# Flamingo cross-attention with a mixture-of-experts FFN: PV in pairs, four P buffers, scores apart, V in halves

## Chip, cores and metric

One core of one Trainium2 chip. The metric is the device time of one execution in microseconds (us), as the median of the runs.

## What is computed

Sixteen batch entries of 56 queries attend to 1500 context keys of width 128 in 16 heads of 8 lanes; then a gated residual, and an FFN with 8 routed experts (top 2) and a shared one.

```python
q = layernorm(x) @ qw.T + qb;  k = ctx @ kw.T + kb;  v = ctx @ vw.T + vb      # 16 x 56 x 128, 16 x 1500 x 128
scores = einsum('bhqd,bhkd->bhqk', qh * 8 ** -0.5, kh)
scores = where(mask[:, None] == 0, -1e9, scores)
probs = softmax(scores, axis=-1)
x = x + tanh(g_xattn) * (einsum('bhqk,bhkd->bhqd', probs, vh) @ ow.T + ob)
x = x + tanh(g_ffn) * ffn(layernorm(x))          # out / max(|out|), 8 experts, top 2, and a shared one
```

## The kernel before, in words

The program is a written-out order for each engine, with semaphores between them. The attention runs in units k = -1 to 15, one for each batch entry, and each unit works on three entries at once: keys of entry k+2 (`pe_k`, `pe_any`), scores for the row maximum and V of entry k+1 (`pe_score`, `pe_v`, `pe_max_row`), and transposed scores, exponentials and PV of entry k (`pe_scores_t`, `act_exp`, `pe_pv`). The 1500 keys are twelve tiles of 128 (the last of 92), and a unit has twelve steps j, one a tile. PE's order in a unit is `pe_unit`, ScalarE's (ACT) `act_unit`, VectorE's (DVE) `dve_unit`.

- K: three matmuls of 512, 512 and 476 columns into `misc`, the third bank of `ring`. ACT stores each to `k_raw`, GpSimd splits it in two halves of fp16, DMAs lay them in `keys`. `misc` is used in turn for K (steps 0 to 2), any (3), the spread of the sums (`pe_attn`, step 4) and V (steps 5 to 7), and each waits until the one before it is read out.
- Score: 24 matmuls of 112 x 512 (the last eight of 476), fp16, into banks 0 and 1 of `ring` in turn. DVE takes the maximum over each (`dve_max`), so score m waits for maximum m - 2. `S_STEPS` says how many stand in each step: 2, 2, 2, 2, 2, 3, 3, 3, 3, 2, 0, 0.
- st: eight fp16 matmuls of 112 columns, the transposed scores of one tile. ACT's `act_exp` makes P of it in `probs`, with three buffers before.
- PV: `pe_pv` uses the array as four groups of 32 columns. Heads 3g to 3g+2 go to group g as one matmul of 168 columns (the wide ones, the first loop) and head 12+g as one of 56 (the narrow ones, the second loop), all fp32. The tile of step j is multiplied two steps later (`LAG = 2`), one PV in each step; the last two tiles of entry k stand in steps 0 and 1 of unit k+1.
- After PV of an entry DVE reads it out (`dve_norm`, three instructions, step 2), `pe_attn` spreads the sums, `dve_recip` takes the reciprocal (step 4), GpSimd multiplies. V waits for that reciprocal.

Unit 15 has st and PV alone. Behind it in DVE's queue stand `dve_bias`, `dve_split` for four experts and only then the norm of entry 15, on which the projection waits:

```python
            units(dve, dve_unit, {0: add_bias})
            dve_bias(dve)
            for e in range(EARLY):
                dve_split(dve, e)
            dve_norm(dve, (B, B % NB, B // NB))
            dve_recip(dve, (B, B % NB, B // NB))
```

Of the kernel before, what the change touches and what calls it, by code (L numbers as in the profile page):

```python
# [13 lines left out]
P = 128  # L14
# [4 lines left out]
KT = 12  # L19
# [59 lines left out]
def flamingo_kernel(nc, d, out):  # L79

    with ExitStack() as ctx:
# [37 lines left out]
        sums = sb("sums", [P, 2, S])  # L119
        max_part = sb("max_part", [QW, PAIRS, NCH])  # L120
        neg_max = sb("neg_max", [QW, PAIRS], F16)
        probs = sb("probs", [P, 3, HQ])
        recip = sb("recip", [P, 2, S])
        attn = sb("attn", [P, 2, TOK])
        ow_rows = sb("ow_rows", [P, 2, D])
# [96 lines left out]
            return chunk(c).stop - c * CH  # L222


        S_STEPS, at = [], 0
        for n in (2, 2, 2, 2, 2, 3, 3, 3, 3, 2, 0, 0):
            S_STEPS.append(range(at, at + n))
            at += n
        assert at == PAIRS * NCH
# [39 lines left out]
        def pe_k(pe, b, c):  # L269

            k, u, t = b
            w = buf(b, 2)
            if c == 0:
                pe.wait_ge(ctx_loaded[w], 16 * (lap(b, 2) + 1))
                if not known(k, 0):
# [17 lines left out]
        def pe_attn(pe, b):  # L293

            k, u, t = b
            if has(k, 2):
                pe.wait_ge(s["any_done"], k + 3)
            else:
                pe.wait_ge(s["v_stored"], NCH * (k + 1 if k < B else B))
            pe.wait_ge(s["sums_done"], k)  # L300
            for r in range(2):
                mm = nc.tensor.matmul(misc[:, r * S:(r + 1) * S], spread[:, r, :], sums[:, r, :],
                                      start=True, stop=True)
            mm.then_inc(s["spread_made"], 1)

        def pe_v(pe, b, c):

            k, u, t = b
            if c == 0:
                if has(k, -1):  # L310
                    pe.wait_ge(s["recip_done"], k)
# [9 lines left out]
            mm.then_inc(s["v_made"], 1)  # L321

        def pe_score(pe, b, m):

# [38 lines left out]
        def pe_pv(pe, b, j):  # L363
# [8 lines left out]
            for g in range(CG):  # L372
                rows = slice(CW * g, CW * (g + 1))
                nc.tensor.matmul(pv[rows, 0:HG * S], v_ext[0:m, u, j, VW * HG * g:VW * HG * g + CW],  # L374
                                 probs[0:m, j % 3, HG * S * g:HG * S * (g + 1)],
                                 start=(j == 0), stop=(j == KT - 1), skip_group_check=True)
            for g in range(CG):
                rows = slice(CW * g, CW * (g + 1))
                h = WIDE + g
                mm = nc.tensor.matmul(pv[rows, HG * S:(HG + 1) * S], v_ext[0:m, u, j, VW * h:VW * h + CW],  # L380
                                      probs[0:m, j % 3, S * h:S * (h + 1)],
                                      start=False, stop=(j == KT - 1), skip_group_check=True)
            mm.then_inc(s["pv_done"], 1)

        LAG = 2

        def pe_unit(pe, b):
            k, u, t = b
            before = (k - 1, buf(b, -1), None)
            for j in range(KT):  # L390
                if j in K_STEPS and has(k, 2):
                    pe_k(pe, b, K_STEPS.index(j))
                if has(k, 0):
                    pe_scores_t(pe, b, j)
                scores = list(S_STEPS[j]) if has(k, 1) else []
                for m in scores[0:1]:
                    pe_score(pe, b, m)
# [4 lines left out]
                if j in V_STEPS and has(k, 1):  # L402
                    pe_v(pe, b, V_STEPS.index(j))
                for m in scores[1:2]:
                    pe_score(pe, b, m)
                if j >= LAG and has(k, 0):
                    pe_pv(pe, b, j - LAG)
                if j < LAG and has(k, -1):
                    pe_pv(pe, before, KT - LAG + j)
                for m in scores[2:]:  # L410
                    pe_score(pe, b, m)
                if j == TURN_STEP and has(k, 1):
                    pe_max_row(pe, b)

# [117 lines left out]

        def dve_unit(dve, b):
            k, u, t = b
            for j in range(KT):
                if j == 0 and has(k, 2):
                    dve_mask(dve, b)
                if j == NORM_STEP and has(k, -1):
                    dve_norm(dve, b)
                scores = list(S_STEPS[j]) if has(k, 1) else []  # L540
                for m in scores[0:1]:
                    dve_max(dve, b, m)
                if j == ANY_STEP and has(k, 2):
                    dve_any(dve, b)
                for m in scores[1:2]:
                    dve_max(dve, b, m)
                if j == RECIP_STEP and has(k, -1):
                    dve_recip(dve, b)
                for m in scores[2:]:
                    dve_max(dve, b, m)  # L550
                if j == TURN_STEP - 1 and has(k, 1):
                    dve_merge_max(dve, b)


        def pool_keys(pool, b, c):
# [586 lines left out]
```

## Time and profile before

| | us |
|---|---|
| median of three runs | 580.48 (579.09 to 580.92) |
| the profiled execution | 578.95 |
| its span, first to last instruction | 577.1 |
| attention units, unit 0's first K to the last PV | 57.4 to 450.8 |
| one unit (the turn of the row maxima to the next one) | 25.30 |
| after the attention | 457.2 to 577.1 |

The span is what the profiler saw of one execution; the profiled execution's own time is 1.85 us more. A timeline row gives the start and the length of a run of like instructions; the difference of two starts is what PE took from one to the other. Ends of matmuls overlap the next starts, so starts are compared here and not ends. An fp32 matmul of the program shows as two in the trace.

### The profile page before, as it was taken

What the parts mean: (1) busy time and instruction counts of PE and PEld (TensorE: products, weight loads), DVE (VectorE), ACT (ScalarE), POOL (GpSimd) and SP (SyncE); (2) the same over time, 40 slices, a digit from 0 to 9 for tenths busy, and PEclk for the clock granted to TensorE, in tenths of its full rate; (3) what the DMA queues carried; (4) which work ended last, traced back from release to release, by engine and by line L of the source; (5) the groups of instructions that cost most, each with busy time, mean ns of one, the idle gap of its engine ahead of it and who ended that gap; (6) DMA issues with size and microseconds to landing.
All of it is one profiled execution on the core that took longest, in us unless ns stands there. A gap on an engine that the chain in (4) does not pass through costs nothing.

```text
span 577.1 us, 15690 instructions
## 1 busy us (share of the span) xinstructions
PE 509.8 (88%) x6779; PEld 353.5 (61%) x6779; DVE 399.5 (69%) x753; ACT 330.3 (57%) x411; POOL 140.5 (24%) x128
## 2 busy tenths in 40 slices
PE   1365999999999999999999999999899469999993
PEld 1123667676766767676676767667677355777772
DVE  6357567687766768776776878677674556778756
ACT  2211566656566665656666565665657228788781
POOL 4051514325061432506153250605000000000000
PEclk9869899999999999999999999999999768999997
DMA  4999869886686867668586766847000500210001
GB/s 151 197 246 243 176 167 178 218 184 134 151 190 150 172 152 185 131 153 185 150 173 156 175 136 156 183 84 163 3 3 2 147 0 2 71 42 2 1 2 32
DMA packets 39805, 72.82 MB, mean 126 GB/s; under 512 B 4638, under 2 KB 26271, under 8 KB 39736
## 3 DMA queue, kind: packets, MB, share of 16 engines
q1 hardware_dynamic: 38456, 70.90, 54.1%
q10 hardware_dynamic: 1280, 0.92, 0.7%
q8 instruction: 53, 0.87, 0.7%
q14 instruction: 16, 0.13, 0.1%
HBM read 24.28 MB, written 0.46 MB: 43 GB/s over the span
## 4 chain that ended last, share of the span: by engine, by line
PE 75%; DVE 12%; DMA 5%; issue 4%; ACT 2%; SPq 1%; POOL 1%; ACTq 0%; POOLq 0%; DVEq 0%
PE ring L336 14%; PE pv L374 12%; PE st L357 11%; PE ring L281 9%; PE ring L319 8%; PE st L661 7%; DVE max_part L501 7%; PE ring L700 5%; DMA ctxT<-in_ctx 3%; PE pv L380 3%; DVE recip L530 2%; DMA ident_h<-in_c_ident_h 2%; PE pv L700 1%; SPq L265 1%; PE ring L909 1%
## 5 line engine op out<-in xcount | busy, mean ns | idle before, releaser
L501 DVE TENSOR_REDUCE max_part<-ring 112x1 f32<-112x512 f32 (+1 forms) x384 | 245.3, 673 | 104.2 <-PE ring L336 102.5
L454 ACT ACTIVATE probs<-st 128x896 f32<-128x896 f32 x192 | 175.6, 915 | 104.1 <-PE st L357 101.3
L336 PE MATMUL ring<-keys,qrs 121*112 121x512 f16 (+1 forms) x384 | 141.2, 392 | 8.4 <-DVE max_part L501 4.0
L357 PEld LDWEIGHTS st<-qrs,keys 121*128 121x128 f16 (+1 forms) x1536 | 89.7, 102 | 42.9 <-issue 13.9
L357 PE MATMUL st<-qrs,keys 121*128 121x112 f16 (+1 forms) x1536 | 108.8, 214 | 2.0 <-ACT qrs L443 2.0
L561 POOL TENSOR_TENSOR k_hi<-k_raw,zero 128x512 f16<-128x512 f32 (+1 forms) x45 | 45.9, 1019 | 219.6 <-ACT k_raw L422 219.0
L374 PE MATMUL pv<-probs,v_ext 128*32 128x168 f32 (+1 forms) x1536 | 94.5, 318 | 0.3 <-DVE sums L521 0.2
L281 PE MATMUL ring<-ctxT,w_qkv 128*128 128x512 f32 (+1 forms) x94 | 56.5, 688 | 13.3 <-DMA ctxT<-in_ctx 13.1
L336 PEld LDWEIGHTS ring<-keys,qrs 121*112 121x112 f16 x384 | 46.6, 131 | 32.2 <-DVE max_part L501 26.2
L374 PEld LDWEIGHTS pv<-probs,v_ext 128*32 128x32 f32 (+1 forms) x1536 | 30.3, 108 | 46.3 <-issue 33.8
L422 ACT ACTIVATE k_raw<-ring,biases 128x512 f32<-128x512 f32 (+1 forms) x45 | 30.5, 677 | 46.3 <-PE ring L281 44.7
L683 DVE TENSOR_TENSOR keys<-probs,keys 128x896 f16<-128x896 f32 x36 | 39.3, 1091 | 24.6 <-ACT keys L678 24.5
L319 PE MATMUL ring<-w_qkv,ctxT 128*128 128x128 f32 (+1 forms) x384 | 52.0, 278 | 4.3 <-DVE recip L530 4.3
L319 PEld LDWEIGHTS ring<-w_qkv,ctxT 128*128 128x128 f32 (+1 forms) x384 | 48.9, 189 | 9.1 <-DVE recip L530 8.5
L380 PE MATMUL pv<-probs,v_ext 128*32 128x56 f32 (+1 forms) x1536 | 54.2, 213 | 0.0
L380 PEld LDWEIGHTS pv<-probs,v_ext 128*32 128x32 f32 (+1 forms) x1536 | 50.0, 110 | 4.7
L564 POOL TENSOR_TENSOR k_lo<-k_raw,k_hi 128x512 f16<-128x512 f32 (+1 forms) x45 | 51.1, 1135 | 3.5
L661 PE MATMUL st<-keys 128*128 128x512 f16 x216 | 48.8, 366 | 0.5 <-DVE score L1011 0.5
L670 ACT ACTIVATE probs<-st,up_bias 128x896 f32<-128x896 f32 x36 | 36.2, 1007 | 16.7 <-PE st L661 16.7
L434 ACT ACTIVATE v_ext<-ring 128x512 f32<-128x512 f32 (+1 forms) x48 | 27.4, 571 | 24.1 <-PE ring L319 24.1
L700 PE MATMUL ring<-keys 128*128 128x128 f16 x612 | 40.0, 219 | 0.9 <-DVE keys L683 0.9
L700 PEld LDWEIGHTS ring<-keys 128*128 128x128 f16 x612 | 36.3, 98 | 6.5 <-DVE keys L683 1.0
(113 smaller groups left out, 374.4 us busy)
## 6 DMA issues: line engine op xcount, KB each, us to landing
ctxT<-in_ctx SPq DMA_DIRECT2D x16, 750.0 KB, 4.2
keys<-mask_add SPq DMA_DIRECT2D x32, 375.0 KB
keys<-k_hi SPq DMA_DIRECT2D x32, 375.0 KB, 6.1
keys<-k_lo SPq DMA_DIRECT2D x32, 375.0 KB, 7.0
keys<-mask_add SPq DMA_DIRECT2D x32, 281.2 KB
mask_raw<-in_mask SPq DMA_DIRECT2D x15, 375.0 KB, 3.7
up_w<-in_up_w SPq DMA_DIRECT2D x9, 256.0 KB, 2.8
down_w<-in_down_w SPq DMA_DIRECT2D x9, 256.0 KB, 3.2
```

Source lines behind the costliest of these rows:

```text
L281: nc.tensor.matmul((first_k[c] if known(k, -1) else misc)[:, 0:width(c)], w_qkv[:, 1, :], ctxT[:, w, chunk(c)], start=True, stop=True).the ...
L319: mm = nc.tensor.matmul(misc[0:m, i * P:(i + 1) * P], ctxT[:, buf(b, 1), j * P:j * P + m], w_qkv[:, 2, :], start=True, stop=True)
L336: nc.tensor.matmul(ring[0:QW, m % 2, 0:width(c)], qrs[0:ROWS, w, p, :, :].rearrange("r h q -> r (h q)"), keys[0:ROWS, w, p, chunk(c)], sta ...
L357: mm = nc.tensor.matmul(st[0:m, j % 2, p // 4, QW * (p % 4):QW * (p % 4 + 1)], keys[0:ROWS, u, p, j * P:j * P + m], qrs[0:ROWS, u, p, :, : ...
L374: nc.tensor.matmul(pv[rows, 0:HG * S], v_ext[0:m, u, j, VW * HG * g:VW * HG * g + CW], probs[0:m, j % 3, HG * S * g:HG * S * (g + 1)], sta ...
L380: mm = nc.tensor.matmul(pv[rows, HG * S:(HG + 1) * S], v_ext[0:m, u, j, VW * h:VW * h + CW], probs[0:m, j % 3, S * h:S * (h + 1)], start=F ...
L454: nc.scalar.activation(probs[0:m, j % 3, :].rearrange("p (h c) -> p h c", h=2), st[0:m, j % 2, :, 0:HQ // 2], ACT.Exp).then_inc(s["exps_do ...
L501: nc.vector.tensor_reduce(max_part[:, p, c:c + 1], ring[0:QW, m % 2, 0:width(c)], AX.X, ALU.max).then_inc(s["max_read"], 1)
L561: nc.gpsimd.tensor_tensor(k_hi[:, chunk(c)], k_raw[:, chunk(c)], zero[:, :].to_broadcast([P, width(c)]), ALU.add).then_inc(s["k_hi_made"], 1)
L564: nc.gpsimd.tensor_tensor(k_lo[:, chunk(c)], k_raw[:, chunk(c)], k_hi[:, chunk(c)], ALU.subtract).then_inc(s["k_lo_made"], 1)
L661: mm = nc.tensor.matmul(st[:, n % 2, h, 0:cols], split_w[e][:, 0, w, c * P:(c + 1) * P], xn_p[:, x, 4 * P * h:4 * P * h + cols], start=(i ...
L700: mm = nc.tensor.matmul(down_banks[e % 2][t // 4][:, P * (t % 4):P * (t % 4 + 1)], hid[:, n % HR, x, P * t:P * (t + 1)], split_w[e][:, 1, ...
```

## The change

`probs` gets a fourth buffer. PV is issued two tiles at a time in the odd steps: steps 3 to 11 take tiles j-3 and j-2, and step 1 the last two of the entry before. Inside one PV the eight matmuls are mixed: wide on groups 0 and 1, narrow on 2 and 3, then wide on 2 and 3, narrow on 0 and 1 (tile 0 keeps wide before narrow). Each V step is cut in two halves, and a table `S_ORDER` puts a single score at each of 24 places between other blocks. V moves from steps 5 to 7 to steps 4 to 6, the spread (`pe_attn`) from step 4 to step 8. DVE's norm moves behind the maxima of step 1, its reciprocal behind those of step 8, and the mask of the next unit is written at the end of a unit.

```diff
-        probs = sb("probs", [P, 3, HQ])
+        probs = sb("probs", [P, 4, HQ])
...
-        for n in (2, 2, 2, 2, 2, 3, 3, 3, 3, 2, 0, 0):
+        S_ORDER = ((0, 0), (0, 1), (1, 0), (1, 1), (1, 4), (2, 0), (2, 1), (3, 1), (3, 4), (4, 1), (4, 2), (4, 3),
...
-        K_STEPS, ANY_STEP, ATTN_STEP, V_STEPS, TURN_STEP = (0, 1, 2), 3, 4, (5, 6, 7), 11
-        NORM_STEP, RECIP_STEP = 2, 4
+        K_STEPS, ANY_STEP, V_STEPS, ATTN_STEP, TURN_STEP = (0, 1, 2), 3, (4, 5, 6), 8, 11
+        NORM_STEP, RECIP_STEP = 1, 8
...
-        def pe_v(pe, b, c):
+        def pe_v(pe, b, c, half):
...
-            if c == 0:
-                if has(k, -1):
-                    pe.wait_ge(s["recip_done"], k)
-                elif has(k, 2):
+            if c == 0 and not half:
+                if has(k, 2):
                     pe.wait_ge(s["any_done"], k + 3)
-            else:
+                else:
+                    pe.wait_ge(s["recip_done"], k - 1)
+            elif not half:
                 pe.wait_ge(s["v_stored"], NCH * (k + 1) + c)
-            for i in range(4):
+            for i in range(2 * half, 2 * half + 2):
...
+            first = [(g, 0) for g in range(CG)] + [(g, 1) for g in range(CG)]
+            for g, last in first if j == 0 else PV_ORDER:
...
+        PV_ORDER = ((0, 0), (1, 0), (2, 1), (3, 1), (2, 0), (3, 0), (0, 1), (1, 1))
...
+        def pe_pv_pair(pe, b, j):
+
+            k, u, t = b
+            if j % 2 and j > LAG and has(k, 0):
+                for i in (j - LAG - 1, j - LAG):
+                    pe_pv(pe, b, i)
+            if j == LAG - 1 and has(k, -1):
+                for i in range(KT - LAG, KT):
+                    pe_pv(pe, (k - 1, buf(b, -1), None), i)
...
+                pe_slot(pe, b, j, 1)
...
+                if j in V_STEPS:
+                    if has(k, 1):
+                        pe_v(pe, b, V_STEPS.index(j), 0)
+                    pe_slot(pe, b, j, 2)
+                    if has(k, 1):
+                        pe_v(pe, b, V_STEPS.index(j), 1)
+                pe_slot(pe, b, j, 3)
+                pe_pv_pair(pe, b, j)
+                pe_slot(pe, b, j, 4)
```

PE, step 7 of a full unit before, with the last score of step 6 ahead of it (`ring<-keys,qrs` is a score, `ring<-w_qkv,ctxT` V, `st` the transposed scores):

```order
L336 MATMUL ring<-keys,qrs 112x512
L357 MATMUL st<-qrs,keys 128x112 x8
L336 MATMUL ring<-keys,qrs 112x476
L319 MATMUL ring<-w_qkv,ctxT 128x128 x3
L319 MATMUL ring<-w_qkv,ctxT 92x128
L336 MATMUL ring<-keys,qrs 112x476
L374 MATMUL pv<-probs,v_ext 32x168 x4
L380 MATMUL pv<-probs,v_ext 32x56 x4
L336 MATMUL ring<-keys,qrs 112x476
```

The same V block now stands in step 6, with the pair of step 7 behind it:

```order
L359 MATMUL st<-qrs,keys 128x112 x8
L338 MATMUL ring<-keys,qrs 112x512
L320 MATMUL ring<-w_qkv,ctxT 128x128 x2
L338 MATMUL ring<-keys,qrs 112x476
L320 MATMUL ring<-w_qkv,ctxT 128x128
L320 MATMUL ring<-w_qkv,ctxT 92x128
L338 MATMUL ring<-keys,qrs 112x476
L359 MATMUL st<-qrs,keys 128x112 x8
L378 MATMUL pv<-probs,v_ext 32x168 x2
L378 MATMUL pv<-probs,v_ext 32x56 x2
```

The third V block is cut by a score, and step 6 has no PV any more; it stands in step 7 together with that step's own, as four runs of two wide and two narrow matmuls for each tile.

DVE, a full unit before, from its mask to its merge of the maxima (`max_part` is a maximum over one score):

```order
L476 TENSOR_SCALAR mask_add<-mask_raw 128x750
L478 TENSOR_REDUCE mask_abs<-mask_raw 128x1
L483 TENSOR_SCALAR any_row<-c_rows,mask_abs 128x56
L501 TENSOR_REDUCE max_part<-ring 112x1 x4
L519 TENSOR_TENSOR own_pv<-pv,c_f 128x168
L521 COPY sums<-pv 128x56
L523 TENSOR_REDUCE sums<-own_pv 128x56
L501 TENSOR_REDUCE max_part<-ring 112x1 x3
L492 SCALAR_TENSOR_TENSOR any_key<-ring,halves 128x112
L501 TENSOR_REDUCE max_part<-ring 112x1 x3
L530 RECIPROCAL recip<-ring 128x112
L501 TENSOR_REDUCE max_part<-ring 112x1 x14
```

And now:

```order
L491 TENSOR_SCALAR mask_add<-mask_raw 128x750
L493 TENSOR_REDUCE mask_abs<-mask_raw 128x1
L498 TENSOR_SCALAR any_row<-c_rows,mask_abs 128x56
L516 TENSOR_REDUCE max_part<-ring 112x1 x5
L534 TENSOR_TENSOR own_pv<-pv,c_f 128x168
L536 COPY sums<-pv 128x56
L538 TENSOR_REDUCE sums<-own_pv 128x56
L516 TENSOR_REDUCE max_part<-ring 112x1 x3
L507 SCALAR_TENSOR_TENSOR any_key<-ring,halves 128x112
L516 TENSOR_REDUCE max_part<-ring 112x1 x13
L545 RECIPROCAL recip<-ring 128x112
L516 TENSOR_REDUCE max_part<-ring 112x1 x3
```

The norm stands one maximum later, the reciprocal ten maxima later; the mask stays between the merge and the first maximum of a unit.

PE, unit 15 before, its fourth PV and the spread of entry 14's sums (`ring<-sums,c_f`):

```order
L374 MATMUL pv<-probs,v_ext 32x168 x4
L380 MATMUL pv<-probs,v_ext 32x56 x4
L357 MATMUL st<-qrs,keys 128x112 x8
L302 MATMUL ring<-sums,c_f 128x56 x2
L374 MATMUL pv<-probs,v_ext 32x168 x4
```

And now, from the last matmuls of its fourth pair:

```order
L378 MATMUL pv<-probs,v_ext 32x168 x2
L378 MATMUL pv<-probs,v_ext 32x56 x2
L359 MATMUL st<-qrs,keys 128x112 x8
L303 MATMUL ring<-sums,c_f 128x56 x2
L359 MATMUL st<-qrs,keys 128x112 x8
```

Before, the spread stands behind five st and four PV; now behind nine st and eight PV.

## Rows read from the trace of the kernel before

**Rows 1.** The page, part 1: busy time of PE.

```profile
PE 509.8 (88%) x6779; PEld 353.5 (61%) x6779; DVE 399.5 (69%) x753; ACT 330.3 (57%) x411; POOL 140.5 (24%) x128
```

**Rows 2.** The page, part 4: the chain that ended last, by engine.

```profile
PE 75%; DVE 12%; DMA 5%; issue 4%; ACT 2%; SPq 1%; POOL 1%; ACTq 0%; POOLq 0%; DVEq 0%
```

**Rows 3.** The table by stretches, one unit: length, busy us (x instructions), clock, DMA.

```profile
208.69:233.99 25.30, 24.69 (x368) 16.92 (x359) 18.59 (x34) 15.48 (x21) 8.78 (x8) 1.00 0.72 162
```

**Rows 4.** The timeline of PE in that unit: start, length, what.

```profile
208.69 0.56 PE L344 MATMUL ring<-ident_h,neg_max 112*1 112x112 f16 x8
...
214.13 1.06 PE L281 MATMUL ring<-ctxT,w_qkv 128*128 128x476 f32 x2
215.03 0.56 PE L357 MATMUL st<-qrs,keys 121*128 121x112 f16 x8
215.43 0.60 PE L336 MATMUL ring<-keys,qrs 121*112 121x512 f16 x2
215.96 0.49 PE L374 MATMUL pv<-probs,v_ext 128*32 128x168 f32 x8
...
220.31 0.38 PE L336 MATMUL ring<-keys,qrs 121*112 121x512 f16 x1
221.01 1.16 PE L319 MATMUL ring<-w_qkv,ctxT 128*128 128x128 f32 x8 [0.31 <-DVE recip L530]
222.00 0.38 PE L336 MATMUL ring<-keys,qrs 121*112 121x512 f16 x1
...
228.63 0.92 PE L336 MATMUL ring<-keys,qrs 121*112 121x476 f16 x2
229.48 0.49 PE L374 MATMUL pv<-probs,v_ext 128*32 128x168 f32 x8
...
232.02 0.57 PE L357 MATMUL st<-qrs,keys 121*128 121x112 f16 x8
232.52 0.49 PE L374 MATMUL pv<-probs,v_ext 128*32 128x168 f32 x8
...
233.04 0.59 PE L357 MATMUL st<-qrs,keys 121*92 121x112 f16 x8
...
233.99 0.56 PE L344 MATMUL ring<-ident_h,neg_max 112*1 112x112 f16 x8
```

**Rows 5.** The timeline of PE where one PV follows another.

```profile
449.04 0.49 PE L374 MATMUL pv<-probs,v_ext 128*32 128x168 f32 x8
...
449.45 0.47 PE L374 MATMUL pv<-probs,v_ext 128*32 128x168 f32 x8
449.74 0.28 PE L380 MATMUL pv<-probs,v_ext 128*32 128x56 f32 x8
```

**Rows 6.** The timeline of PE at the end of unit -1.

```profile
53.98 0.27 PE L893 MATMUL pv<-ow_rows,biases 128*1 128x128 f32 x1
54.02 0.26 PE L344 MATMUL ring<-ident_h,neg_max 112*1 112x112 f16 x2
```

**Rows 7.** The timelines of DVE (four rows) and ACT (one) in the unit of rows 4.

```profile
214.71 0.32 DVE L519 TENSOR_TENSOR own_pv<-pv,c_f 128x168 f32<-128x168 f32 x1
...
215.19 0.35 DVE L523 TENSOR_REDUCE sums<-own_pv 128x56 f32<-128x168 f32 x1
215.85 1.29 DVE L501 TENSOR_REDUCE max_part<-ring 112x1 f32<-112x512 f32 x2 [0.31 <-PE ring L336]
...
222.42 0.69 DVE L501 TENSOR_REDUCE max_part<-ring 112x1 f32<-112x512 f32 x1 [0.93 <-PE ring L336]
...
222.20 0.60 ACT L434 ACTIVATE v_ext<-ring 128x512 f32<-128x512 f32 x1 [0.77 <-PE ring L319]
```

**Rows 8.** The timelines in and behind unit 15: st of tile 0, DVE, PE.

```profile
436.61 0.57 PE L357 MATMUL st<-qrs,keys 121*128 121x112 f16 x8 [1.02 <-ACT qrs L443]
...
441.99 0.86 DVE L530 RECIPROCAL recip<-ring 128x112 f32<-128x112 f32 x1 [2.36 <-PE ring L302]
...
457.15 1.08 PE L302 MATMUL ring<-sums,c_f 128*128 128x56 f32 x4 [6.45 <-DVE sums L523]
```

More of the change, by code:

```diff
@@ L222, in width @@
             return chunk(c).stop - c * CH
[L225 to L229 removed]
+        S_ORDER = ((0, 0), (0, 1), (1, 0), (1, 1), (1, 4), (2, 0), (2, 1), (3, 1), (3, 4), (4, 1), (4, 2), (4, 3),
+                   (5, 2), (5, 3), (5, 4), (6, 1), (6, 2), (6, 3), (7, 4), (8, 1), (8, 3), (9, 1), (9, 4), (10, 1))
+        S_SLOTS = {place: (m,) for m, place in enumerate(S_ORDER)}
+        S_STEPS = [[m for m, place in enumerate(S_ORDER) if place[0] == j] for j in range(KT)]
         SCORES = PAIRS * NCH
[L231 to L232 removed]
+        K_STEPS, ANY_STEP, V_STEPS, ATTN_STEP, TURN_STEP = (0, 1, 2), 3, (4, 5, 6), 8, 11
+        NORM_STEP, RECIP_STEP = 1, 8
         def sp_load_ctx(sp, k, u):
@@ L274, in pe_k @@
                 pe.wait_ge(ctx_loaded[w], 16 * (lap(b, 2) + 1))
-                if not known(k, 0):
+                if has(k, -2):
+                    pe.wait_ge(s["recip_done"], k - 1)
+                elif not known(k, 0):
                     pe.wait_ge(s["v_stored"], NCH * (k + 1))
@@ L320, in pe_v @@
                                       w_qkv[:, 2, :], start=True, stop=True)
-            mm.then_inc(s["v_made"], 1)
+            if half:
+                mm.then_inc(s["v_made"], 1)
         def pe_score(pe, b, m):
@@ L377, in pe_pv @@
[L377 to L382, printed above, removed]
+                h, n = (WIDE + g, 1) if last else (HG * g, HG)
+                mm = nc.tensor.matmul(pv[rows, last * HG * S:last * HG * S + n * S],
+                                      v_ext[0:m, u, j, VW * h:VW * h + CW],
+                                      probs[0:m, j % 4, S * h:S * (h + n)],
+                                      start=(j == 0 and not last), stop=(j == KT - 1), skip_group_check=True)
@@ L383, in pe_pv, with pe_slot @@
             mm.then_inc(s["pv_done"], 1)
+        PV_ORDER = ((0, 0), (1, 0), (2, 1), (3, 1), (2, 0), (3, 0), (0, 1), (1, 1))
         LAG = 2
+        def pe_pv_pair(pe, b, j):
[6 more added lines that the diff above has]
+                    pe_pv(pe, (k - 1, buf(b, -1), None), i)
+        def pe_slot(pe, b, j, x):
+            if has(b[0], 1):
+                for m in S_SLOTS.get((j, x), ()):
+                    pe_score(pe, b, m)
@@ L387, in pe_unit @@
         def pe_unit(pe, b):
             k, u, t = b
-            before = (k - 1, buf(b, -1), None)
             for j in range(KT):
-                if j in K_STEPS and has(k, 2):
-                    pe_k(pe, b, K_STEPS.index(j))
+                if j in K_STEPS:
+                    if has(k, 2):
+                        pe_k(pe, b, K_STEPS.index(j))
+                    pe_slot(pe, b, j, 0)
                 if has(k, 0):
                     pe_scores_t(pe, b, j)
-                scores = list(S_STEPS[j]) if has(k, 1) else []
-                for m in scores[0:1]:
-                    pe_score(pe, b, m)
+                pe_slot(pe, b, j, 1)
@@ L401, in pe_unit @@
                     pe_attn(pe, b)
[L402 to L411, printed above, removed]
+                if j in V_STEPS:
+                    if has(k, 1):
+                        pe_v(pe, b, V_STEPS.index(j), 0)
+                    pe_slot(pe, b, j, 2)
+                    if has(k, 1):
+                        pe_v(pe, b, V_STEPS.index(j), 1)
+                pe_slot(pe, b, j, 3)
+                pe_pv_pair(pe, b, j)
+                pe_slot(pe, b, j, 4)
                 if j == TURN_STEP and has(k, 1):
@@ L534, in dve_unit @@
             k, u, t = b
+            if known(k, 0):
+                dve_mask(dve, b)
             for j in range(KT):
-                if j == 0 and has(k, 2):
-                    dve_mask(dve, b)
+                if j == ANY_STEP and has(k, 1):
+                    dve_max(dve, b, S_STEPS[j][0])
+                if j == ANY_STEP and has(k, 2):
+                    dve_any(dve, b)
+                for m in S_STEPS[j][j == ANY_STEP:] if has(k, 1) else ():
+                    dve_max(dve, b, m)
                 if j == NORM_STEP and has(k, -1):
                     dve_norm(dve, b)
[L540 to L546, printed above, removed]
                 if j == RECIP_STEP and has(k, -1):
                     dve_recip(dve, b)
-                for m in scores[2:]:
-                    dve_max(dve, b, m)
                 if j == TURN_STEP - 1 and has(k, 1):
                     dve_merge_max(dve, b)
+            if has(k, 3):
+                dve_mask(dve, (k + 1, buf(b, 1), lap(b, 1)))
         def pool_keys(pool, b, c):
```

16 lines of the change are left out of this document (6 added, 10 removed).

## Prediction

> **What bounds the kernel now.** I read the page's busy shares first: PE is busy 88% of the span, DVE 69%, ACT 57% [rows 1]. The chain that ended last says the same of the path: 75% of it is PE, 12% DVE, 5% DMA [rows 2]. So a unit of the attention is PE's queue from end to end, and what changes its length is what PE's queue takes, not what DVE or ACT are busy with. The table by stretches gives the room: one unit is 25.30 us, PE is busy 24.69 of it at a granted clock of 1.00, DVE 18.59, ACT 15.48, GpSimd 8.78, and the DMA share is 0.72 [rows 3]. No other engine has less than 6.7 us of slack. But "busy 24.69" hides two things that only the timeline shows, and the change works on both: the taxes that PE pays when it goes into and out of PV, and the waits on DVE inside a pair of scores and ahead of V. Nearly all of the gain or loss is therefore the difference of one unit, times some fifteen.
>
> **PV in pairs.** A PV between two st takes 0.52 us from its start to the next st (232.52 to 233.04), and the st ahead of it takes 0.50 (232.02 to 232.52), where an st ahead of a score takes 0.40 (215.03 to 215.43) [rows 4]. So going in costs 0.10. A PV that follows a PV is seen once in this trace without a wait: 0.41 from start to start (449.04 to 449.45) [rows 5]. Its parts are 0.29 for the two wide rounds (449.45 to 449.74) and so 0.12 or less for the narrow ones [rows 5]. Joining two PVs saves 0.52 - 0.41 = 0.11 at the exit and 0.10 at the entry, 0.21 for each of six pairs: **1.26 us a unit**. The four column groups have the same load in the mixed order (one wide and one narrow each), so I cost the new order of the eight matmuls at nothing. This holds if the groups run each at its own pace. The end of unit -1 shows that they do: the eight matmuls L344 stand ahead of L893 in the program, on another column group, and yet the first L893 starts at 53.98 and two of the L344 only at 54.02 [rows 6]. The bounds of a join are 0.52 (nothing saved at the exit, 0.60 a unit left) and 0.38 (no slack at all, 1.4 a unit).
>
> The Trainium skill ("TensorE: Matmul & The Clock Gate", Part 3, What overlaps and what doesn't) states the opposite of these rows: matmuls start and end in strict program order. By that rule a narrow matmul's second half would wait behind a wide one's, and the mixed order would lose part of the join; by the rows it loses nothing. The sum would be 563 by the rule (the first rival below works it out) and is 555 by the rows. The trace of unit -1 speaks against the rule, and I go by the trace.
>
> **Scores apart.** Two scores in front of a PV take 0.53 without a wait (215.43 to 215.96), which is 0.32 for the second with PV's entry and 0.21 to 0.22 for the first. The late pairs of 476 columns would take 0.50 but take 0.85 (228.63 to 229.48), because the second waits until DVE has read the bank [rows 4]. That is 0.35, twice a unit: **0.70 us**. In the new order such neighbours are at least an st (0.40), half of V (some 0.45 of the block's 0.99) or a K apart. DVE needs 0.60 from one maximum to the next (two in 1.29, one of them 0.69) [rows 7], and a score with an st is 0.62, so DVE keeps up.
>
> **V and the reciprocal.** The first V waits for the reciprocal: 0.70 from the score to V (220.31 to 221.01) instead of 0.22 [rows 4]. Now V waits for nothing of DVE but `any_key`, and the next K for the reciprocal, which stands 3 us and more ahead: **0.48 us** gone. Two waits are new. (a) The second V, at the head of step 5, needs the first one stored. ACT starts that 0.20 after the block's end (222.00 to 222.20) and takes 0.60 [rows 4, 7], with some 0.05 to hand over 0.85; PE has only a score and an st between, 0.62. Wait 0.24. (b) The norm stands behind the maximum of score (1, 4). With t as that score's start, its maximum starts at 0.46 (0.42 as at 222.00 to 222.42, and 0.04 for coming out of PV), the norm at 1.06, and lasts 0.83 (214.71 to 215.54) less 0.06 of overlap, so the maximum of (2, 0) runs from 1.83 to 2.52 [rows 4, 7]. PE reaches (3, 1), which needs that bank, at 0.26 + 0.90 (the third K, 214.13 to 215.03) + 0.22 + 0.40 + 0.22 + 0.40 = 2.40; with the hand-over it waits some 0.21 [rows 4]. The reciprocal behind (8, 3) has a score, an st and a pair of PV after it and costs at most 0.05. The wait of the first K's successor for the row maxima stays as it is: the first score takes it in place of the first st.
>
> **Sum of a unit.** 1.26 + 0.70 + 0.48 - 0.24 - 0.21 = **1.99 us**, from 25.30 to 23.3. PE then is busy nearly throughout, and DVE has 18.59 of 23.3: still room. GpSimd's keys and the DMAs behind them start as late in the unit as before (the third K about 5 us in) and are needed at the next one's first score; that slack shrinks by 2 us, and I cost it at nothing. The fourth P buffer is what lets ACT write tile j while j-3 to j-1 wait; it costs no instruction.
>
> **All units.** Thirteen full ones (1 to 13): 25.9. Unit 0 has five pairs and no wait for a reciprocal to lose, unit 14 has no K, so that its scores come closer together: I take 1.4 for each. That is 28.7.
>
> **What the change gives back.** In unit 15 the spread now waits for nine st and eight PV instead of five and four. Before, the reciprocal starts 5.38 after the first st (436.61 to 441.99) [rows 8], of which five st and four single PV are 5 x 0.40 + 4 x 0.62 = 4.48, so 0.90 is the rest. Now it is 9 x 0.40 + 4 x (0.10 + 0.41 + 0.52) + 0.90 = 8.62: **3.2 us later**. DVE's bias, its four splits and entry 15's norm stand behind that reciprocal, and PE waits for them at the end, idle for 6.45 us before 457.15 [rows 8]. So PE's shorter unit 15 gains nothing and the whole 3.2 is paid. The bounds are 0 (the splits wait for DMAs that come no later) and 3.6.
>
> Start and FFN are left as they are: unit 0 begins when its context has landed.
>
> **The sum**: -28.7 + 3.2 = -25.5, on the profiled execution's 578.95 gives 553.5. The median of the runs lies 1.5 above that execution, so the forecast for the median is **555.0 us**, 4.4% less. The likeliest case's own range is 549 to 561: a join between 0.38 and 0.44, the two new waits between half and double.
>
> **Rivals.**
> - *The groups keep program order.* Then the narrow second half on groups 2 and 3 starts with the wide one on 0 and 1, 0.14 late, and a pair ends some 0.09 later: 6 x 0.09 x 15.5 = 8.4 us, **563**. For it: nothing in this trace but the regular starts; against it: rows 6. Chance 0.10. This is what the page named above would make of it.
> - *DVE becomes the bound of the steps around norm and reciprocal.* If the maxima that stand behind them cannot catch up in the pair of PV that follows, their 0.83 and 0.85 fall on PE whole, 1.7 a unit against 0.25 in my sum: 1.4 x 14 = 20 us, **575**; half of that is likelier. For it: DVE's share goes from 0.73 to 0.80, and each bank is read 1.1 us after its score starts. Against it: the norm has a K, the reciprocal a pair behind it. Chance 0.13.
> - *Slower: wide and narrow do not run side by side.* The place is the mixed PV. If a round lasted as long as the wide and then the narrow part one after the other, a PV would stream twice its 0.38 us. There are 176 such PVs (16 x 11), so from 25.5 / 176 = 0.145 us more for each the gain is gone; at the full 0.38 it is 67 us, **622**. For it: the trace has no PV in which groups differ in width. Against it: rows 6 again, where groups go on alone. Chance 0.04.
> - *The change does not do what it says*: the pair waits for exponentials and P buffers as the singles do, so that no join happens, and only the scores gain: 0.7 x 15 less 3.2, **572**. Against it: a pair in step j takes tiles j-3 and j-2, whose exponentials are one and two steps old. Chance 0.03.
>
> **How the numbers follow.** The forecast has 0.70. A difference of 0.3% (1.7 us) is about what runs of this kernel tell apart, so faster by more than that holds in the forecast, in the first, second and fourth case: 0.94. Slower takes the third and a little for a wait that I do not see: 0.04. Same 0.02. For 8 in 10 the range takes the likeliest's own, the 563 and the milder half of the DVE case: 548 to 567.
>
> **What would show it.** The turn of row maxima repeats every 23.3 us (before 25.30). PV following PV is 0.41 behind it, twelve PVs have six entries. No score waits 0.35 for a maximum; the second V waits 0.2 to 0.3; (3, 1) waits 0.2. In unit 15 the reciprocal starts 8.6 after the first st and PE's idle time ahead of the last spread grows from 6.45 to about 11. The prediction is wrong if a PV inside a pair takes over 0.5, if DVE shows fewer idle gaps than a unit of 23.3 leaves, or if PE waits for a K's keys at the first score.

## The result and the profile after

The changed kernel takes **548.82 us** (548.20 to 549.51, four runs) against 580.48 for the kernel before; the ratio is 0.9459, with a 95% interval of 0.9438 to 0.9480. It is 5.4% faster where 4.4% was forecast (555.0), 0.8 above the low end of the range (548) and just below the likeliest case's own 549 to 561. The profiled execution took 548.36 us, 30.6 less than the one before.

The page of the changed kernel, part 1 and the chain of part 4, to be held against [rows 1] and [rows 2]:

```profile
PE 484.0 (89%) x6779; PEld 358.9 (66%) x6779; DVE 398.9 (73%) x753; ACT 328.4 (60%) x411; POOL 139.5 (26%) x128
...
PE 77%; DVE 7%; issue 5%; DMA 5%; ACT 3%; SPq 1%; POOL 1%; ACTq 0%; POOLq 0%; DVEq 0%
```

Every engine runs as many instructions as before, and DVE is busy for the same 399 us. DVE's part of the chain has gone from 12% to 7%, and PE is busy for 25.8 us less: both PE's own work and the waits on DVE have shrunk. One unit in the table by stretches (columns as in [rows 3]):

```profile
241.75:264.74 22.99, 22.78 (x365) 17.25 (x355) 18.53 (x34) 15.39 (x21) 8.69 (x8) 1.00 0.81 178
```

25.30 became 23.00, 2.30 less where 1.99 was forecast. The timeline of PE in this unit (start, length, what), the first ten rows from its steps 0 to 3, then two of step 5, then three of step 7:

```profile
242.24 1.12 PE L282 MATMUL ring<-ctxT,w_qkv 128*128 128x512 f32 x2
243.40 0.39 PE L338 MATMUL ring<-keys,qrs 121*112 121x512 f16 x1
...
244.24 1.02 PE L282 MATMUL ring<-ctxT,w_qkv 128*128 128x512 f32 x2
245.10 0.38 PE L338 MATMUL ring<-keys,qrs 121*112 121x512 f16 x1
...
246.02 0.98 PE L378 MATMUL pv<-probs,v_ext 128*32 128x168 f32 x32
246.93 0.42 PE L338 MATMUL ring<-keys,qrs 121*112 121x512 f16 x1
247.19 0.96 PE L282 MATMUL ring<-ctxT,w_qkv 128*128 128x476 f32 x2
247.99 0.38 PE L338 MATMUL ring<-keys,qrs 121*112 121x512 f16 x1
...
248.82 0.56 PE L359 MATMUL st<-qrs,keys 121*128 121x112 f16 x8
249.47 0.42 PE L338 MATMUL ring<-keys,qrs 121*112 121x512 f16 x1
...
252.96 0.55 PE L359 MATMUL st<-qrs,keys 121*128 121x112 f16 x8
253.60 0.71 PE L320 MATMUL ring<-w_qkv,ctxT 128*128 128x128 f32 x4
...
258.19 0.56 PE L359 MATMUL st<-qrs,keys 121*128 121x112 f16 x8
258.68 0.97 PE L378 MATMUL pv<-probs,v_ext 128*32 128x168 f32 x32
259.58 0.41 PE L338 MATMUL ring<-keys,qrs 121*112 121x476 f16 x1
```

A pair is one row of 32 matmuls: 0.91 from its start to the next score, entry 0.09 ahead of it (st to pair 0.49 against st to score 0.40). The two new waits are the ones that the sum had: score (3, 1) starts 0.65 after its st (248.82 to 249.47), 0.26 late, and the second V 0.64 after its st (252.96 to 253.60), 0.24 late. The old wait for the row maxima is still there: the first score starts 1.16 after the first K (242.24 to 243.40), where the first st started 1.09 after it before. The other two K are shorter than before: the third takes 0.80 (247.19 to 247.99) where it took 0.90 [rows 4], and the second 0.86 where it took 0.97. The timeline of PE in the unit of [rows 4], its first two K and the st behind each:

```profile
209.18 1.13 PE L281 MATMUL ring<-ctxT,w_qkv 128*128 128x512 f32 x2
210.27 0.57 PE L357 MATMUL st<-qrs,keys 121*128 121x112 f16 x8
...
211.72 1.12 PE L281 MATMUL ring<-ctxT,w_qkv 128*128 128x512 f32 x2
212.69 0.56 PE L357 MATMUL st<-qrs,keys 121*128 121x112 f16 x8
```

Unit 15 and the end, DVE's and PE's timelines, to be held against [rows 8]:

```profile
402.23 0.56 PE L346 MATMUL ring<-ident_h,neg_max 112*1 112x112 f16 x8
403.79 0.96 PE L359 MATMUL st<-qrs,keys 121*128 121x112 f16 x16 [1.00 <-ACT qrs L458]
...
412.42 0.86 DVE L545 RECIPROCAL recip<-ring 128x112 f32<-128x112 f32 x1 [5.85 <-PE ring L303]
...
425.96 1.07 PE L303 MATMUL ring<-sums,c_f 128*128 128x56 f32 x4 [9.38 <-DVE sums L538]
```

The reciprocal starts 8.63 after the first st, forecast 8.62, before 5.38. The time from there to the last spread is 13.54 (before 15.16), and PE's idle time ahead of it has gone from 6.45 to 9.38, where about 11 was forecast.

Stretch by stretch, from starts in the two traces:

| stretch | before | after | difference | forecast |
|---|---|---|---|---|
| to unit 0's first K | 57.4 | 56.6 | -0.9 | 0 |
| unit 0 | 24.8 | 24.0 | -0.8 | -1.4 |
| units 1 to 13 | 328.9 | 299.2 | -29.7 | -25.9 |
| unit 14 | 23.9 | 22.5 | -1.5 | -1.4 |
| to unit 15's reciprocal | 7.0 | 10.2 | +3.2 | +3.2 |
| from there to the last spread | 15.2 | 13.5 | -1.6 | 0 |
| projection and FFN | 120.0 | 120.6 | +0.7 | 0 |

### The profile page after: what moved, and what is told of

Its sections match the earlier page's. It is cut to its first block, busy times and chain, and to the rows that moved or that the text cites. A ratio compares the mean times of both kernels' runs of the same rounds, so it can differ in the third digit from the quotient of the medians.

```text
span 546.6 us, 15689 instructions
## 1 busy us (share of the span) xinstructions
PE 484.0 (89%) x6779; PEld 358.9 (66%) x6779; DVE 398.9 (73%) x753; ACT 328.4 (60%) x411; POOL 139.5 (26%) x128
## 4 chain that ended last, share of the span: by engine, by line
PE 77%; DVE 7%; issue 5%; DMA 5%; ACT 3%; SPq 1%; POOL 1%; ACTq 0%; POOLq 0%; DVEq 0%
PE ring L338 16%; PE pv L378 15%; PE st L359 11%; PE ring L320 8%; PE st L675 8%; PE ring L282 7%; PE ring L714 6%; DMA ctxT<-in_ctx 3%; DVE max_part L516 2%; ACT v_ext L449 2%; DMA ident_h<-in_c_ident_h 2%; PE pv L714 1%; SPq L264 1%; PE ring L346 1%; PE ring L923 1%
## 5 line engine op out<-in xcount | busy, mean ns | idle before, releaser
L469 ACT ACTIVATE probs<-st 128x896 f32<-128x896 f32 x192 | 172.2, 916 | 71.2 <-PE st L359 68.9
L338 PE MATMUL ring<-keys,qrs 121*112 121x512 f16 (+1 forms) x384 | 150.1, 393 | 6.8 <-DVE max_part L516 3.0
L359 PEld LDWEIGHTS st<-qrs,keys 121*128 121x128 f16 (+1 forms) x1536 | 97.2, 102 | 30.2 <-issue 9.5
L378 PE MATMUL pv<-probs,v_ext 128*32 128x168 f32 (+3 forms) x3072 | 93.6, 262 | 0.1
L378 PEld LDWEIGHTS pv<-probs,v_ext 128*32 128x32 f32 (+1 forms) x3072 | 73.1, 109 | 21.6 <-issue 11.1
L338 PEld LDWEIGHTS ring<-keys,qrs 121*112 121x112 f16 x384 | 50.1, 131 | 41.7 <-DVE max_part L516 17.7
L320 PE MATMUL ring<-w_qkv,ctxT 128*128 128x128 f32 (+1 forms) x384 | 60.0, 278 | 1.7 <-ACT v_ext L449 0.5
L320 PEld LDWEIGHTS ring<-w_qkv,ctxT 128*128 128x128 f32 (+1 forms) x384 | 56.2, 188 | 6.4 <-ACT v_ext L449 4.4
L697 DVE TENSOR_TENSOR keys<-probs,keys 128x896 f16<-128x896 f32 x36 | 39.3, 1090 | 24.9 <-ACT keys L692 24.8
L596 POOL TENSOR_TENSOR attn<-sums,recip 128x112 f32<-128x112 f32 x16 | 7.1, 445 | 175.9 <-DVE recip L545 166.1
L587 POOL TENSOR_TENSOR qrs<-queries,any_key 121x896 f16<-121x896 f16 x16 | 30.2, 1888 | 22.1 <-DMA queries<-probs 22.1
```

The costliest lines, as they stand in the source:

```text
L338: nc.tensor.matmul(ring[0:QW, m % 2, 0:width(c)], qrs[0:ROWS, w, p, :, :].rearrange("r h q -> r (h q)"), keys[0:ROWS, w, p, chunk(c)], sta ...
L359: mm = nc.tensor.matmul(st[0:m, j % 2, p // 4, QW * (p % 4):QW * (p % 4 + 1)], keys[0:ROWS, u, p, j * P:j * P + m], qrs[0:ROWS, u, p, :, : ...
L378: mm = nc.tensor.matmul(pv[rows, last * HG * S:last * HG * S + n * S], v_ext[0:m, u, j, VW * h:VW * h + CW], probs[0:m, j % 4, S * h:S * ( ...
L469: nc.scalar.activation(probs[0:m, j % 4, :].rearrange("p (h c) -> p h c", h=2), st[0:m, j % 2, :, 0:HQ // 2], ACT.Exp).then_inc(s["exps_do ...
L697: nc.vector.tensor_tensor(hid[:, n % HR, 1, :], hid_raw[n % 3], hid[:, n % HR, 0, :], ALU.subtract).then_inc(s["hid_lo_done"], 1)
```

## Experiments

Every kernel was timed against the kernel before on the same chip (578.6 to 578.9 there); the ratio stands beside its time. A unit is the distance of two turns of the row maxima in the one execution that was profiled; but for one or two units of some kernels (the last section) it repeats within 0.01 us, so it tells apart what the total can't.

**The order inside PV.**

```diff
-            for g, last in first if j == 0 else PV_ORDER:
+            for g, last in first:
```

> The changed kernel with the eight matmuls of every PV in the old order, four wide and then four narrow. A pair in the changed kernel takes 0.905 us from its first matmul to what follows, where 0.407 + 0.521 = 0.928 was expected of joined PVs. Theory A (the column groups run on their own; the mixed order hides a part of the first load): a pair takes 0.928, 0.023 more, six a unit, some 15.5 units: 2.1 us slower than the changed kernel, about 551. Theory B (the groups keep program order, so mixing costs 0.09 a pair): the pair gets shorter, 0.81, and the kernel 8 us faster, about 540. Theory C (order is worth nothing, the 0.023 is from elsewhere): pair 0.905, 549.

549.60 us, ratio 0.9493 (0.9465 to 0.9521). Its unit is 23.00, as in the changed kernel, and so is its pair (the timeline of PE):

```profile
245.78 0.98 PE L378 MATMUL pv<-probs,v_ext 128*32 128x168 f32 x32
246.69 0.42 PE L338 MATMUL ring<-keys,qrs 121*112 121x512 f16 x1
```

The two totals aren't told apart by their intervals; the unit and the pair are what decide. Theory C holds: the mixed order is worth nothing, and costs nothing. Theory B falls with it: a kernel in which the groups keep program order would have got shorter. That the pair is 0.905 and not 0.928 lies in the second PV: 0.41 is the first one's, and the second takes 0.50 and not the 0.52 of a lone PV. Its wide rounds take 0.29 (449.45 to 449.74 [rows 5]) where a lone PV's take 0.31 in the kernel before. Why a PV behind another is 0.02 shorter was not tested.

**Pairs alone**, in the kernel before.

```diff
-                if j >= LAG and has(k, 0):
-                    pe_pv(pe, b, j - LAG)
-                if j < LAG and has(k, -1):
-                    pe_pv(pe, before, KT - LAG + j)
+                if j % 2 and j > LAG and has(k, 0):
+                    for i in (j - LAG - 1, j - LAG):
+                        pe_pv(pe, b, i)
+                if j == LAG - 1 and has(k, -1):
+                    for i in range(KT - LAG, KT):
+                        pe_pv(pe, before, i)
```

(and four P buffers, as in the change)

> The kernel before with only the pairs and the fourth P buffer: old places of scores, V in one block, old order inside PV, reciprocal at step 4. Theory A (entry and exit of PV are the larger part): six joins at 0.207 and 0.10 for the one K that no longer follows a PV save 1.34 us a unit; the scores then stand closer in even steps and wait more for DVE, which I put at 0.5: 0.85 net, 13 us, about 567. No 3.2 us is paid at the end. Theory B (isolated scores are what gives; joined PVs starve DVE and the gain is eaten): 575 or more.

585.49 us, ratio 1.0102 (1.0072 to 1.0133): slower than the kernel before, the unit 25.77. Theory A (567) is wrong. Theory B (575 or more) holds, though its words, that the gain is eaten, fall short of a loss. The joins are there, and the waits are larger than what they save. PE's timeline in one unit:

```profile
222.48 0.38 PE L336 MATMUL ring<-keys,qrs 121*112 121x512 f16 x1
223.79 1.16 PE L319 MATMUL ring<-w_qkv,ctxT 128*128 128x128 f32 x8 [0.94 <-DVE recip L532]
...
227.77 0.60 PE L336 MATMUL ring<-keys,qrs 121*112 121x512 f16 x2
228.20 0.56 PE L357 MATMUL st<-qrs,keys 121*128 121x112 f16 x8
...
231.90 0.92 PE L336 MATMUL ring<-keys,qrs 121*112 121x476 f16 x2
233.01 0.41 PE L336 MATMUL ring<-keys,qrs 121*112 121x476 f16 x1 [0.19 <-DVE max_part L503]
```

V waits 1.31 behind its score for the reciprocal (before 0.70, [rows 4]), since no PV stands between any more in the even step; and the two scores of step 8 take 1.11 from the start of the first to the next one behind them (231.90 to 233.01), where two that wait for nothing take 0.43 (227.77 to 228.20). Against the kernel before, V's wait has grown by 0.6, and four other waits (two scores in step 3, one in step 6, those of step 8) by 0.25 to 0.35 each: 1.9 in all, against the 1.38 that the joins save. A PV between scores had been cover for DVE. Taking it away in every other step makes DVE the bound there.

**Places alone**: the changed kernel with one PV in each step.

```diff
-            if j % 2 and j > LAG and has(k, 0):
-                for i in (j - LAG - 1, j - LAG):
-                    pe_pv(pe, b, i)
-            if j == LAG - 1 and has(k, -1):
-                for i in range(KT - LAG, KT):
-                    pe_pv(pe, (k - 1, buf(b, -1), None), i)
+            if j >= LAG and has(k, 0):
+                pe_pv(pe, b, j - LAG)
+            if j < LAG and has(k, -1):
+                pe_pv(pe, (k - 1, buf(b, -1), None), KT - LAG + j)
```

> The changed kernel with one PV in each step, two steps behind, instead of pairs; four P buffers, scores, V halves and mixed order as changed. Theory A: six entries and exits come back, 6 x (0.207 + 0.023) = 1.38 us a unit, two K stand behind a PV again, 0.20, and the wait of the second V (0.24) is covered by step 4's PV: 1.35 a unit, 21 us, about 570. Theory B (the scores' places give all, pairs little): under 555.

564.02 us, ratio 0.9721 (0.9687 to 0.9755), unit 24.00. PE's timeline where the changed kernel has its two waits:

```profile
234.92 0.57 PE L359 MATMUL st<-qrs,keys 121*128 121x112 f16 x8
235.33 0.38 PE L338 MATMUL ring<-keys,qrs 121*112 121x512 f16 x1
...
238.48 0.59 PE L378 MATMUL pv<-probs,v_ext 128*32 128x168 f32 x16
239.01 0.57 PE L359 MATMUL st<-qrs,keys 121*128 121x112 f16 x8
239.41 0.67 PE L320 MATMUL ring<-w_qkv,ctxT 128*128 128x128 f32 x4
```

Neither is there: the score follows its st at 0.41, V at 0.40. Of the K, only the second stands behind a PV here (230.01 to 230.97, 0.96; in the changed kernel 0.86); the third already stands behind a score (232.68 to 233.48) and takes 0.80 in both, so the expectation counted one K too many. Between this kernel and the changed one lie six joins and one K (1.38 + 0.10) less the two waits (0.50): 0.98, and 1.00 is measured. Theory A named the mechanism, and besides the K it missed the wait of (3, 1), which a PV in step 2 covers too. Taken together, a unit is 25.30 with neither, 24.00 with the places (of scores, V, norm and reciprocal together), 25.77 with the pairs, 23.00 with both: the pairs are worth 1.00 with the new places and cost 0.47 without them.

**The spread of unit 15 early**, at step 4 as before the change, in that unit alone.

```diff
-                if j == ATTN_STEP and has(k, -1):
+                if j == (4 if k == B - 1 else ATTN_STEP) and has(k, -1):
...
-                if j == RECIP_STEP and has(k, -1):
+                if j == (4 if k == B - 1 else RECIP_STEP) and has(k, -1):
```

> The changed kernel with the spread and the reciprocal of unit 15 alone at step 4, as before the change; nothing else moved. Theory A (DVE's bias, splits and last norm hang on that reciprocal, so the 3.2 us that it came later are paid in full): PE's last spread starts 3.2 us earlier behind the last row-maxima turn, 545.6. Theory B (the splits wait for their weights' DMAs, which come no sooner): under 1 us gained, 548 to 549.

544.54 us, ratio 0.9392 (0.9370 to 0.9415), 0.0067 or 3.9 us below the changed kernel. The profile gives 3.3 of it in its place: DVE's and PE's timelines,

```profile
409.50 0.86 DVE L545 RECIPROCAL recip<-ring 128x112 f32<-128x112 f32 x1 [2.06 <-PE ring L303]
...
423.52 1.07 PE L303 MATMUL ring<-sums,c_f 128*128 128x56 f32 x4 [6.07 <-DVE sums L538]
```

put the reciprocal 6.40 behind that kernel's last turn of the row maxima (403.10) instead of 10.19, and the last spread 20.42 behind it instead of 23.73. Theory A holds.

**One score ahead of the second V** instead of behind step 5's pair.

```diff
-                   (5, 2), (5, 3), (5, 4), (6, 1), (6, 2), (6, 3), (7, 4), (8, 1), (8, 3), (9, 1), (9, 4), (10, 1))
+                   (5, 1), (5, 2), (5, 3), (6, 1), (6, 2), (6, 3), (7, 4), (8, 1), (8, 3), (9, 1), (9, 4), (10, 1))
```

> The changed kernel with one score moved from behind step 5's pair (5, 4) to between step 5's st and the second V (5, 1). In the changed kernel that V starts 0.634 after its st instead of 0.39 and its first half takes 0.549 instead of 0.444. Theory A (the wait is the store of the first V, and any 0.22 of other work covers it): 0.22 to 0.35 us a unit, a unit of 22.65 to 22.8 instead of 23.00, 3 to 5 us. Theory B (without the score behind the pair DVE gets three maxima close together and one after a gap, and the wait moves to a score): unit 22.95 to 23.1, no change.

545.14 us, ratio 0.9414 (0.9393 to 0.9434), unit 22.75. Theory A at its lower end: V follows the score 0.25 behind, nearly without a wait.

**The norm one maximum later.**

```diff
-        NORM_STEP, RECIP_STEP = 1, 8
+        NORM_STEP, RECIP_STEP = 2, 8
...
-                for m in S_STEPS[j][j == ANY_STEP:] if has(k, 1) else ():
+                for m in S_STEPS[j][j == ANY_STEP:][0:1] if has(k, 1) else ():
                     dve_max(dve, b, m)
                 if j == NORM_STEP and has(k, -1):
                     dve_norm(dve, b)
+                for m in S_STEPS[j][j == ANY_STEP:][1:] if has(k, 1) else ():
+                    dve_max(dve, b, m)
```

> The changed kernel with the norm one maximum later on DVE, behind that of score (2, 0) instead of (1, 4). In the changed kernel score (3, 1) starts 0.654 after its st, 0.26 late. Theory A (it waits for the maximum that stands behind the norm): the wait is gone, unit 22.72, 4 us faster. Theory B (the norm's 0.74 must fall somewhere between two scores here; the first PV of the next pair, which waits until pv is read out, or the first V, which waits for any_key, takes it over): unit 22.95 to 23.1.

546.72 us, ratio 0.9440 (0.9426 to 0.9454), unit 22.83, 0.17 less. The intervals don't tell its total from the changed kernel's; the unit does. PE's timeline:

```profile
249.62 0.56 PE L359 MATMUL st<-qrs,keys 121*128 121x112 f16 x8
250.01 0.38 PE L338 MATMUL ring<-keys,qrs 121*112 121x512 f16 x1
250.23 0.19 PE L291 MATMUL ring<-any_row,ones_h 128*128 128x56 f16 x1
250.40 0.97 PE L378 MATMUL pv<-probs,v_ext 128*32 128x168 f32 x32
```

The wait of (3, 1) is gone (0.39 behind its st). The gain lies between the two theories, as some of it comes back the way theory B has it: the pair follows `any` at 0.17 instead of 0.12, and the score behind the first half of V at 0.49 instead of 0.45.

**Three P buffers** in the changed kernel (`probs` of three, `j % 3`, and the exponential waits for `pv_done` of tile j - 3).

> The changed kernel with three P buffers. An exponential of an odd step then starts behind the first PV of that step's pair. Theory A (the fourth buffer is needed: step 5's exponential is held up to its pair, ACT stands before the store of the second V, and the third V waits for it): 0.5 us a unit, 8 us slower than the changed kernel. Theory B (ACT has slack enough): under 1 us.

559.56 us, ratio 0.9671 (0.9649 to 0.9693), unit 23.78, 0.78 more. ACT's timeline shows it:

```profile
261.88 0.92 ACT L469 ACTIVATE probs<-st 128x896 f32<-128x896 f32 x1 [2.31 <-PE pv L378]
262.69 0.59 ACT L449 ACTIVATE v_ext<-ring 128x512 f32<-128x512 f32 x1
```

The exponential of step 5 waits 2.31 for the first PV of its pair, the store of V behind it in ACT's queue waits with it, and the third V starts 0.63 after its score. That is theory A, and its 0.5 is right for this place: 0.41 of wait, and 0.11 that the first half behind it takes more. The other 0.27 of the 0.78 lies at the first score, which starts 1.43 after the first K instead of 1.16: ACT copies the row maxima behind the exponentials that are held up. Pairs work with three buffers too, but against the singles' unit of 24.00 they are then worth 0.22 instead of 1.00.

**The three together** (score moved, norm later, spread of unit 15 at step 4).

> The changed kernel with the moved score, the later norm and the early spread of unit 15 together. Theory A (three separate waits): 0.22 to 0.35 and 0.26 a unit and 3.3 us at the end, 537 to 538. Theory B (the two waits in the unit are one slack of DVE, only one of them can be had): 541 or more.

540.62 us (538.18 to 542.52), ratio 0.9332 (0.9301 to 0.9363), unit 22.59. Of the 0.25 and 0.17 that they gave alone, 0.41 is there: separate waits, as theory A has it. The total alone would not say so: it came out some 3 us above the 537 to 538 of A, near the 541 of B, with executions 4.3 us apart; the profiled one, the fastest, has 538.18.

**The spread at step 2** in that kernel (`2 if k == B - 1` in both places).

> The combined kernel with the spread and the reciprocal of unit 15 at step 2, right behind the norm, instead of step 4. Between the two places PE has two st and a pair of PV, 1.7 us. Theory A (the end hangs on that reciprocal alone): 1.5 to 2 us faster than the combined kernel, the reciprocal 4.3 to 4.8 us behind the last row-maxima turn instead of 6.2. Theory B (from here on the weights' DMAs or the last PVs set the end): no change.

538.70 us, ratio 0.9315 (0.9294 to 0.9337), not told apart from the kernel before it by the intervals. In the profile the reciprocal of unit 15 starts 5.15 behind the last turn of the row maxima instead of 6.39, 1.24 and not the 1.5 to 2 expected, and PE's idle time ahead of the last spread falls again, from 6.60 to 3.84 (PE's timeline):

```profile
416.44 0.62 PE L303 MATMUL ring<-sums,c_f 128*128 128x56 f32 x4 [3.84 <-DVE sums L538]
```

From the last turn to that spread the two profiles differ by 2.2 us; but in this one unit 0's first K comes 2.5 later (59.29 against 56.83), which hides it in the totals. That K lies anywhere from 56.6 to 59.3 in the twelve profiles, so a difference of some 2 us between two single executions can come from the start alone. It is the lowest time found, 6.9% below the kernel before and 1.5% below the changed one by their ratios.

**V whole** in the changed kernel.

```diff
                         pe_v(pe, b, V_STEPS.index(j), 0)
-                    pe_slot(pe, b, j, 2)
-                    if has(k, 1):
                         pe_v(pe, b, V_STEPS.index(j), 1)
+                    pe_slot(pe, b, j, 2)
```

> The changed kernel with both halves of each V block together and the score that stood between them right behind, so that two scores are neighbours in steps 4, 5 and 6. Theory A (neighbouring scores wait for DVE, 0.35 for each such pair as before the change): 0.35 to 1.0 us a unit, unit 23.4 to 24.0, 5 to 15 us slower than the changed kernel. Theory B (only the late pairs of the kernel before waited, since three scores in a step were too many for DVE; here two are not): unit 23.0, under 2 us.

547.07 us, ratio 0.9443 (0.9418 to 0.9468), unit 22.78: shorter than the changed kernel's, though the intervals don't tell the totals apart. Theory A falls; B is right that no score waits, and its unit of 23.0 was still too high. PE's timeline:

```profile
252.68 1.05 PE L320 MATMUL ring<-w_qkv,ctxT 128*128 128x128 f32 x8
253.57 0.60 PE L338 MATMUL ring<-keys,qrs 121*112 121x512 f16 x2
254.01 0.56 PE L359 MATMUL st<-qrs,keys 121*128 121x112 f16 x8
254.43 1.16 PE L320 MATMUL ring<-w_qkv,ctxT 128*128 128x128 f32 x8
```

Two scores side by side take 0.44 together, no wait; DVE has had a whole V block to catch up, which would explain it. And V, which ends one score earlier, is stored sooner, so that the next V waits 0.02 instead of 0.24. The halves gain nothing; they bring one of the two new waits.

## Why the prediction was right, and where it was off

**The bound.** Right: PE's queue is the path, and the gain is PE's: 2.30 of a unit.

**Pairs, 1.26.** Right in kind; the size is 6 x 0.23 = 1.38, 0.12 more, as the second PV of a pair takes 0.50 and not 0.52. What the sum did not say is that this gain exists only beside the new places: alone the pairs cost 0.47 a unit. The rival "DVE becomes the bound of steps" is what happens in that kernel; in the changed one it stays at the 0.26 of (3, 1).

**K.** The step that was missing. A K right behind a PV takes 0.10 longer, which I did not see, as I took PV's exit from PV to st and to scores only. Two of the three K stand behind a score now and take 0.86 and 0.80 instead of 0.97 and 0.90: 0.2 a unit. The kernel with single PVs shows both cases at once, 0.96 for its K behind a PV and 0.80 for the one behind a score. Against this, the wait for the row maxima behind the first K, which the sum left as it is, grew by 0.07 (1.09 to 1.16). So K gives 0.13 net, 2 us in all.

**Scores apart, 0.70, and V's wait for the reciprocal, 0.48.** Both waits are gone from the trace. The single-PV kernel, which has the new places and no pairs, gives 1.30 of a unit: 0.70 + 0.48 + 0.10 for the third K, which no longer follows a PV, less 0.09 for the wait behind the first (1.18 there) make 1.19 of it. How the 1.30 divides between the scores and V is read from the timelines; no run moves one without the other. That scores must stand alone was not so: V whole puts two side by side without a wait. As far as these runs show, what matters is how many maxima DVE has to take between two gaps.

**The new waits, 0.24 and 0.21.** Measured 0.24 and 0.26, at the named places, and the moved score and the later norm take them away (0.25 and 0.17 a unit). Beside the wait, the V that waits is itself 0.10 or 0.11 longer: the first block before (0.99 against 0.89), the first half of the second V now (0.55 against 0.44). The two cancel. With the score moved that half still takes 0.54 (276.35 to 276.89), so the cause is open.

**The unit in all.** 1.99, and 0.12 for the pairs, 0.13 for K, less 0.05 for the new waits, make 2.19. The other 0.11 of the 2.30 lies in small terms that rows rounded to 0.01 don't sort out; the largest one found is the pair behind `any`, which pays 0.03 going in (0.12 from `any` to the pair, 0.09 from `any` to a score before) and not 0.10.

**What the change gives back, 3.2.** Right to 0.1 at its place, and shown by the early spread (on DVE the reciprocal stands eleven maxima later than before, not ten). The bound of 0 for "the splits wait for DMAs" was not idle: from the reciprocal to the last spread it took 15.2 in the kernel before and in the one with pairs alone, and 13.1 to 14.6 in the ten others, 1.6 less in the changed kernel. DVE's timeline says where the 1.6 lies, two rows of the kernel before and two of the changed one:

```profile
449.79 0.43 DVE L628 TENSOR_SCALAR keys<-up_w 128x512 f16<-128x512 f32 x1 [0.32 <-DMA up_w<-in_up_w]
453.81 0.43 DVE L628 TENSOR_SCALAR keys<-up_w 128x512 f16<-128x512 f32 x1 [1.60 <-DMA up_w<-in_up_w]
...
420.11 0.43 DVE L642 TENSOR_SCALAR keys<-up_w 128x512 f16<-128x512 f32 x1 [0.21 <-DMA up_w<-in_up_w]
421.16 0.43 DVE L644 TENSOR_SCALAR keys<-down_w 128x512 f16<-128x512 f32 x1 [0.62 <-DMA down_w<-in_down_w]
```

The splits of the third and fourth expert wait for their weights' DMAs, 2.68 in all before (0.32, 0.36, 1.60, 0.40) and 1.15 now (0.21, 0.62, 0.32). Without these waits the stretch takes 12.4 to 12.5 in all twelve kernels. So the sum had a wait in this stretch that it put at no change, and it shrank by 1.5. Why the weights come sooner behind their splits with the new places was not tested.

**The rivals.** Program order inside PV (563) and wide beside narrow (622) fall with the pair of 0.905 in either order. "No join" (572; its own terms, 0.7 x 15 less 3.2 off 580.5, give 573) falls with the timeline. What the Trainium skill states in "TensorE: Matmul & The Clock Gate", Part 3, on strict order of matmuls differs from [rows 6] here, and the mixed order brought no loss.

**The numbers.** 548.82 lies in the range and 6.2 below the forecast. The profiled execution came 5.1 below the 553.5 forecast for it: 3.8 from units 1 to 13, 1.6 from the splits and 0.9 from the start, less 0.6 that unit 0 gained too little and 0.7 in projection and FFN. The 0.9 of the start is not an effect that these runs can show, as unit 0's first K lies anywhere from 56.6 to 59.3 in the twelve profiles. The last 1.0 is the step from the profiled execution to the median, 0.5 here where the sum took 1.5.

## What to carry to other kernels

Price a block of another shape at every neighbour, not at one: a PV in 32-column groups costs 0.10 going in, and a K right behind it takes another 0.10. Grouping such work saves the taxes but takes away the cover that it gave another engine's queue; here that was worth more than the taxes (25.30 to 25.77), and they paid only once scores and V had new places (24.00 to 23.00). And when a step moves within a loop, look at its last turn by itself: a reciprocal that nothing in the loop waited for held up other work by 3 us behind the loop.

## What was not expected of the hardware

Matmuls on different column groups pass one another in the changed kernel too, ahead of the units. The timeline of PE, with L346 ahead of L907 in the program:

```profile
53.20 0.37 PE L907 MATMUL pv<-ow_rows,biases 128*1 128x128 f32 x1
53.28 0.30 PE L346 MATMUL ring<-ident_h,neg_max 112*1 112x112 f16 x1
```

In seven of the twelve kernels PE stands still once or twice in the profiled execution behind the pair of step 9, for 0.2 to 1.0 us. It is always in unit 5, and in two kernels (the early spread, the moved score) again in unit 10: unit 5 takes 23.19 in the changed kernel instead of 23.00, and 23.42 in the combined one instead of 22.59. The kernel before, the two with singles or with pairs alone and the one with three buffers show none, and the one in plain order 0.04 in unit 5. In the combined kernel the maximum that the score behind the pair waits for had ended 1.6 us before (190.24 to 191.80). The cause was not tested and stays open, and the fixed places speak against mere chance; it explains under 1.5 us of any total.
